# A decoder's 16-wide-head attentions: where ScalarE takes its second exponential of a slot

## What is computed

```python
x = x + _L0_attn_ref(_layernorm(x), ...)     # 32 heads of 16, sign weights: "gqa" in the kernel
x = x + _L0_xattn_ref(_layernorm(x), ctx, ...)   # heads of 128: "xat"
x = x + _L0_ffn_ref(_layernorm(x), ...)      # "ffn"
x = x + _L1_attn_ref(_layernorm(x), ...)     # 32 heads of 16, alibi: first half of "two"
x = x + _L1_xattn_ref(_layernorm(x), ctx, ctx, ..., mask)   # 32 heads of 16: second half of "two"
x = x + _L1_ffn_ref(_layernorm(x), ...)      # experts: the end of "two"
```

## Time and profile before

| what | value |
|---|---|
| three executions, median | 2241.06 us |
| the profiled execution's own time | 2240.94 us |
| its span | 2239.1 us |
| TensorE busy (matmuls) | 2144.6 us, 96% |
| VectorE busy | 1332.7 us, 60% |
| ScalarE busy | 1042.9 us, 47% |
| GpSimd busy | 903.5 us, 40% |

### The profile page before, as it was taken

The page is one execution under the profiler, slowest core; times in us unless marked ns, Lnnn a source line. Parts: engine busy times, 40 slices in busy tenths (PEclk is TensorE's granted clock), DMA queues, the critical chain, the costliest instruction groups (busy, mean ns, idle before and its releaser), DMA issues. The chain is left out here.

```text
span 2239.1 us, 41017 instructions
## 1 busy us (share of the span) xinstructions
PE 2144.6 (96%) x16686; PEld 1722.5 (77%) x16686; DVE 1332.7 (60%) x2350; ACT 1042.9 (47%) x1778; POOL 903.5 (40%) x675
## 2 busy tenths in 40 slices
PE   6997999999999999999999998999999899999998
PEld 4665877778787787777877777888888677777766
DVE  6985534333343353443334357797886688888866
ACT  6784543544435554354443552111112667777622
POOL 2787241431414413133131336121122668878711
PEclk9998999999999999999999999999999999999999
DMA  4000101101011101100111013000001100100002
GB/s 166 2 21 20 50 27 57 38 31 46 23 54 57 50 27 39 57 25 34 39 38 55 21 64 120 1 0 0 0 0 31 65 2 16 50 26 11 2 1 75
DMA packets 23038, 80.75 MB, mean 36 GB/s; under 512 B 4048, under 2 KB 6224, under 8 KB 16720
## 3 DMA queue, kind: packets, MB, share of 16 engines
q1 hardware_dynamic: 22864, 78.28, 10.1%
HBM read 74.08 MB, written 4.19 MB: 35 GB/s over the span
## 5 line engine op out<-in xcount | busy, mean ns | idle before, releaser
L2618 PE MATMUL xat_TP<-shared_rounded 128*128 128x512 f32 x1024 | 322.5, 396 | 5.8 <-issue 5.8
L2292 POOL TENSOR_TENSOR xat_T<-xat_T,xat_mask 128x512 f32<-128x512 f32 x64 | 81.6, 1298 | 514.2 <-DVE xat_T L2382 514.2
L104 PE MATMUL xat_G<-xat_xnT_hi,shared_rounded 128*128 128x512 f32 x768 | 244.4, 391 | 0.0
L2279 POOL TENSOR_TENSOR shared_rounded<-shared_landing,shared_rounded 128x2048 fp32r<-128x2048 f32 x39 | 179.4, 4610 | 154.7 <-ACT shared_rounded L2136 154.7
L2618 PEld LDWEIGHTS xat_TP<-shared_rounded 128*128 128x128 f32 x1024 | 187.2, 188 | 58.2 <-issue 22.4
L2409 DVE TENSOR_TENSOR X<-X,xat_TP 128x512 f32<-128x512 f32 x128 | 87.0, 680 | 198.3 <-PE xat_TP L2618 198.3
L2618 PE MATMUL xat_TP<-shared_rounded,xat_oT_lo 128*128 128x512 f32 x512 | 199.9, 390 | 0.0
L2373 DVE RECIPROCAL xat_q_inv_rms<-xat_OT 128x16 f32<-128x16 f32 x32 | 8.3, 260 | 312.7 <-PE xat_OT L2545 312.7
L104 PE MATMUL ffn_H<-shared_rounded 128*128 128x448 f32 (+1 forms) x816 | 179.1, 368 | 3.8 <-DVE ffn_h_kept L1445 2.5
L1377 POOL TENSOR_TENSOR ffn_one_hot<-ffn_one_hot,ffn_block_rank 128x448 f32<-128x448 f32 x64 | 75.4, 1179 | 253.9 <-DVE ffn_one_hot L1426 253.9
L1353 ACT ACTIVATE shared_rounded<-ffn_TP 128x384 fp32r<-128x384 f32 x64 | 34.9, 545 | 294.0 <-PE ffn_Y L1502 246.5
(11 more groups left out here) (362 smaller groups left out, 4967.9 us busy)
## 6 DMA issues: line engine op xcount, KB each, us to landing
shared_landing<-in_Cq_q SPq DMA_DIRECT2D x16, 1024.0 KB, 4.8
shared_landing<-in_Cq_o SPq DMA_DIRECT2D x16, 1024.0 KB, 4.7
shared_landing<-in_Cq_kv SPq DMA_DIRECT2D x8, 1024.0 KB, 7.0
shared_landing<-in_ctxT_paired SPq DMA_DIRECT2D x4, 1024.0 KB, 6.9
two_ctxT_raw<-in_ctxT SPq DMA_DIRECT2D x8, 512.0 KB, 4.0
shared_landing<-in_w1T SPq DMA_DIRECT2D x8, 448.0 KB, 4.0
shared_landing<-in_w SPq DMA_DIRECT2D x7, 512.0 KB, 3.6
out<-X SPq DMA_DIRECT2D x6, 512.0 KB, 3.0
```

The costliest lines, as they stand in the source:

```text
L104: last = eng.matmul(out, a, b, start=(n == 0), stop=(n == len(steps) - 1))
L2279: return eng.tensor_tensor(w[1][:, :, :], landed[:, :, :], w[0][:, :, :].bitcast(F32), ALU.subtract)
L2292: eng.tensor_tensor(T[:, n, :, :], T[:, n, :, :], mask[:, :].unsqueeze(1).to_broadcast([P, ROWS, SEQ]), ALU.add)\
L2618: last = eng.matmul(TP[m % 2][:, :], x, w, start=(n == 0), stop=(n == len(steps) - 1))
```

## The change

In ScalarE's program, the exponential of the second unit moves from behind the first one to behind the copy of the slot's second turn. Both calls of `small_attention` are affected. No instruction is added or removed, and the other engines' programs stay as they are.

```diff
                 if 1 <= s < LASTP + 1:
                     exponent(2 * s - 2)
-                    exponent(2 * s - 1)
                 if LAG + 2 <= s < LASTP + LAG + 2 and s % 2 == 1:
                     keep_o((s - LAG - 2) // 2)
                 for item in filled(s, 0):
...
                 if LAG <= s < LASTP + LAG:
                     keep_PT(2 * (s - LAG) + 1)
+                if 1 <= s < LASTP + 1:
+                    exponent(2 * s - 1)
                 for item in filled(s, 0):
                     if item[1] == "k":
                         keep(item)
```

## The result

The changed kernel takes **2244.9 us** (median of 20 runs, 2241.0 to 2249.6), the kernel before 2241.1 (20 runs, 2239.3 to 2243.3). The ratio is 1.0015, with a 95% interval from 1.0009 to 1.0021: slower by 3.7 us where 2.8 less was forecast. The profiled execution took 2245.26 (span 2243.5, mean granted clock 0.991) against 2240.94 (2239.1, 0.993).

What follows compares the result with a forecast made beforehand. TensorE was taken to set the end almost everywhere. Terms -5.2 + 0 + 0.5 + 0 - 0.5 + 2.5 = -2.7 took the profiled 2240.94 to 2238.2, median 2238.3 us; range 2234.5 to 2245.

Steps and rivals of the forecast that it cites:

- rival B: Two's slot 1 margin of 0.13 us fails, TensorE waits in seven groups: 7.7 in all, 2246.0 us; chance 0.11.
- Prices: On ScalarE, one exponential of two in a row costs 0.52 us, so late second copies come 0.52 earlier.
- Part 1, the waits: Gqa's last group, slots 24 to 33: shorter TensorE waits for copies gain 0.15 + 0.52 + 0.52 = 1.2 us.
- Part 1, the clock: Gqa's last group: TensorE's clock stays up after shorter waits, gaining 1.3 us at slot 30 and 2.7 at slot 32.
- the cap by GpSimd: Gqa's slot 28: GpSimd's normalize is ready at 175.94, so the gain up to there is at most 0.15 us.
- Part 2: Gqa's slots 1 to 23: shorter copy waits against later VectorE sums and slot 3's +0.5; 0 us, ends -1 and +1.
- Part 3: Two's start, slot 3: the exponential stands ahead of copies TensorE waits for, +0.5 us.
- Part 4: Two's steady groups: late sums are covered, cost 0; slots 38 and 39 wait less: -0.5 us, ends 0 and -1.
- Part 5: Two's end, slots 62 and 63: late VectorE sums lengthen TensorE's waits, +2.5 us; ends +1 and +4 (longer low clock).
- A: Gqa's last group: the clock still falls after waits of 0.87 and 0.96, total 2242.3 us; chance 0.30.
- C: All 22 TensorE waits for copies shrink by 0.52 and two's end is covered: -11.4, 2229.6 us; chance 0.06.
- D: On ScalarE, copies between exponentials could each cost a table load, over 100 us more; chance 0.01.

Runs made afterwards that it cites:

- e5: New order in gqa's slots 24 to 32 alone, against the kernel before: -3.8 us (-5.8 to -1.8).
- e6: In gqa's slots 24 to 32 both exponentials stand behind the second copy, against the kernel before: -0.2 us (-2.2 to +1.8).

## Why the prediction was wrong, point by point

The trade was understood: every wait that the forecast names moved by what was worked out, to 0.1 us. Two it does not name were added, for the low part of o in gqa's last group and for slot 2's exponential at two's start. The direction was wrong because **the lower clock was booked only on the side of the gains**: -4.0 in part 1, and without that term the forecast's own sum is +1.3. That 2244.9 still lies just inside the stated range (2234.5 to 2245) is luck: its upper end was there for rival B, which did not happen.

- **Prices.** An exponential of one row was put at 0.52: waits of 1.48 became 0.96, and 0.23 became 0.76. Right.
- **Part 1, the waits** (-1.2: 0.15, 0.52 and 0.52). The new order in slots 24 to 32 gives 2.1 in all, of which the turns of slots 28, 30 and 32 in e5 show 0.16, 0.48 and 0.46 (2.43, 1.95 and 1.49 behind the kernel before, from 2.59 at slot 25). Right, the cap by GpSimd too.
- **Part 1, the clock** (-4.0). This term failed. That the clock stays up at slots 26, 30 and 32 was taken from single rows of one profile (0.96 is nearer to the 0.78 of the earlier trace rows than 1.48 is), and the runs do not bear it out. Slot 26's scores vary from 1.21 to 2.01 in either order; slot 30's are 1.21 in two of five new profiles; at slot 32 the product still begins at the lower clock (0.55 in the window above). About 1.0 was left of 4.0 (2.1 less the 1.1 of waits). In e5 it all lies behind slot 32, and there it does repeat, only smaller: from its start to the turn behind it the product takes 2.85 to 3.36 in the seven profiles with the new order, and 3.55 or 3.56 in the eleven others, e6 among them; the turn takes 0.60 in e5 and 1.05 before. A cost was left out beside it: the wait for the low part of o behind the late sum, 0.60 ahead of that product in the changed kernel.
- **Part 2** (0). +0.2 over three profiles: right within its ends. Slot 3's +0.5 is there (1.25 against 0.73 at slot 4), and the shorter waits later give it back.
- **Part 3** (+0.5). The wait was right, and two terms were missing: 0.25 by slot 2's late sum, and the clock. The means differ by 2.0; the 1.2 of it that is the clock may be the draw of these profiles (see the starts).
- **Part 4** (-0.5). -0.2, the same within 0.1 in seven profiles. The cover held in every group: in the changed kernel TensorE's waits for X (L884) in two are 7.2, before 6.6, and its waits for low parts (L243) 3.7, before 4.4.
- **Part 5** (+2.5). The waits were right to 0.1, the clock behind them was left out of the sum, though "a longer low clock" stood at its upper end: +4.5, above that end of +4.
- **Rivals.** A (the clock still falls: 2242.3) was the nearest, and it too took parts 3 and 5 at their waits alone. B did not happen: the margin of 0.13 is 0.17 in the changed kernel, and two's middle gained. C and D did not happen.

From -2.7: +3.1 for part 1's clock, +0.2, +1.5, +0.3 and +2.0 for parts 2 to 5 give the +4.4 of the table.

The trace agrees with the sentence of the Trainium skill that the forecast cited ("TensorE: Matmul & The Clock Gate", Part 1, activity releases the throttled level) only in its direction (longer waits at two's end brought the lower clock in all three profiles that have them, shorter ones ahead of slot 32's product less of it in seven of seven); no row here ties the outcome at a slot to the length of one wait.

## What to carry to other kernels

When a wait grows or shrinks, price the work behind it at both clocks, on the losing side as on the winning side: at two's end 2.5 us of longer waits cost 4.5. Moving one instruction along an engine's program helps only in slots where its old place was the late one, so make such a change by slot: here nine slots of 96 carried the gain and two carried most of the loss. And before a term is built on a row of one profile, ask whether it repeats: cutting several profiles into stretches at fixed instructions resolves 0.1 us where the clock does not differ from one execution to the next (as in two's middle), and medians of 11 runs resolve 2.

## What the hardware showed that was not expected

- The same instructions in the same order ran at different clocks from one execution to the next: the product k of two's start took 3.01, 4.47 and 5.46 in profiles of the order before, which moves the whole by up to 2.8. Ahead of gqa's first sum, where nothing was changed in either, a product of eight took 2.06 before and 3.17 in e5, and that stretch varies from 36.65 to 39.28. Such places are the likely source of the runs' spread; it was not tested apart.
- A clock that stays up can be worth nothing: at gqa's slot 26 the 1.3 us it saves turn into a longer wait for GpSimd at slot 28 in every profile where it happens; with the order before 0.3 of them is left, with the new one nothing (the turn of slot 28 stands 11.8 behind that of slot 25 in the five and the one profile with fast scores, 12.0 to 12.2 and 11.8 in the others).
- The changed kernel's runs spread over 8.6 us, those of the kernel before beside them over 4.0; but 33 runs of the kernel before spread over 6.2 to 9.4 in each of the three larger sets beside the experiments, so the wider spread is no mark of the new order.
